# Moving bias rows and a mean to GpSimd and widening the ring of batches in an attention and ternary feed-forward kernel

## The reference

```python
def ref(x, ctx, Wq, Wk, Wv, Wo, weight, bias):     # x (64, 512, 512), ctx (64, 77, 512)
    x = x + xattn(layernorm(x), ctx, Wq, Wk, Wv, Wo)
    h = layernorm(x)
    w_scale = mean(abs(weight))
    q_weight = sign(weight) * (abs(weight) > 0.5 * w_scale)
    i_scale = max(abs(h)) / 127.0
    q_input = clip(round(h / i_scale), -128.0, 127.0)
    return x + einsum('bsk,ok->bso', q_input, q_weight) * w_scale * i_scale + bias
```

## Time and profile before

| what | value |
|---|---|
| median of three runs | 1105.96 us |
| profiled execution, its own time | 1106.15 us |
| its span, first to last instruction | 1104.4 us |
| TensorE busy | 1075.2 us, 97% |
| VectorE busy | 996.0 us, 90% |
| ScalarE busy | 931.4 us, 84% |
| GpSimd busy | 861.8 us, 78% |
| DMA | 262.94 MB, mean 238 GB/s |
| feed-forward stage | from about 808 us to the end |

### The profile page before, as it was taken

One profiled execution on the slowest core, in us unless ns is written; L12 is line 12 of the kernel. 1 busy time (PEld: TensorE's weight loads), 2 busy tenths in 40 slices (PEclk: granted clock), 3 DMA queues, 4 the chain that ended last, 5 costly groups with the idle time before them and its releaser, 6 DMA issues.

```text
span 1104.4 us, 43628 instructions
## 1 busy us (share of the span) xinstructions
PE 1075.2 (97%) x14065; PEld 867.6 (79%) x14065; DVE 996.0 (90%) x1774; ACT 931.4 (84%) x2081; POOL 861.8 (78%) x1674
## 2 busy tenths in 40 slices
PE   6998999999999999999999999999989999999996
PEld 6997999999999989999999999999745555555552
DVE  4563799999999999999999999999989999999995
ACT  3565799989999999999999999999878888888883
POOL 4675899999999999999999999999844444444442
PEclk9999999999999999999999999999999999999998
DMA  8866267666666766666666753333259999999995
GB/s 281 239 161 207 81 191 218 199 212 202 209 213 191 220 189 215 198 217 204 205 213 190 221 155 115 108 106 107 88 231 364 422 423 425 426 425 404 400 425 225
DMA packets 114615, 262.94 MB, mean 238 GB/s; under 512 B 59913, under 2 KB 71369, under 8 KB 94098
## 3 DMA queue, kind: packets, MB, share of 16 engines
q1 hardware_dynamic: 114002, 262.16, 68.7%
q10 hardware_dynamic: 576, 0.33, 0.1%
HBM read 139.79 MB, written 122.64 MB: 238 GB/s over the span
## 4 chain that ended last, share of the span: by engine, by line
DVE 45%; PE 36%; issue 15%; DVEq 2%; ACT 1%; DMA 0%; POOL 0%; SPq 0%; ACTq 0%; POOLq 0%
DVE x_sb L1110 15%; PE pT_ps L1539 10%; PE sc_ps L1539 10%; DVE mx_sb L1094 9%; DVE bn_sb L1127 6%; DVE bn_sb L1143 6%; PE y_ps L1287 5%; DVE amax L1116 3%; DVE rinv_sb L1088 2%; PE xT_ps L1276 2%; DVE e_sb L1099 2%; PE xT_ps L1525 1%; PE y_ps L1525 1%; PE sc_ps L1548 1%; PE pT_ps L1548 1%
## 5 line engine op out<-in xcount | busy, mean ns | idle before, releaser
L1452 PEld LDWEIGHTS xT_ps<-wqs,xT_sb 128*128 128x128 f32 x2048 | 239.0, 192 | 47.8 <-ACT xT_sb L867 47.7
L1452 PE MATMUL xT_ps<-wqs,xT_sb 128*128 128x128 f32 x2048 | 263.6, 282 | 2.1 <-ACT xT_sb L867 2.1
L741 POOL TENSOR_TENSOR x_sb<-x_sb,mean (+1 forms) x128 | 133.0, 1039 | 154.3 <-DVE q16T_sb L1222 154.3
L1110 DVE SCALAR_TENSOR_TENSOR x_sb<-x_sb,mv_sb,y_ps 128x512 f32 (+1 forms) x252 | 174.9, 735 | 0.1
L1410 PE MATMUL pT_ps<-v_blk,pT_sb 128*128 128x102 f32 (+1 forms) x1280 | 161.5, 273 | 0.2 <-ACT pT_sb L843 0.2
L836 ACT ACTIVATE sq_sb<-x_sb 128x512 bf16 (+1 forms) x256 | 160.7, 628 | 1.0 <-DVE x_sb L1110 0.6
L850 ACT ACTIVATE e_sb<-e_sb,rs_sb 128x308 f32<-128x308 f32 x256 | 127.3, 544 | 36.6 <-DVE e_sb L1099 36.0
L1116 DVE TENSOR_REDUCE amax<-x_sb (+1 forms) x128 | 154.8, 1210 | 0.0
L1410 PEld LDWEIGHTS pT_ps<-v_blk,pT_sb 128*128 128x128 f32 x1280 | 153.2, 192 | 1.0 <-ACT pT_sb L843 1.0
L867 ACT ACTIVATE xT_sb<-xT_ps 128x1024 f32<-128x1024 f32 x128 | 131.2, 1025 | 2.5 <-PE xT_ps L1354 2.4
L1539 PE MATMUL sc_ps<-wT,q16T_sb 64*128 64x512 f16 x1024 | 132.2, 378 | 0.6 <-DVE q16T_sb L1222 0.5
(11 more groups left out here) (155 smaller groups left out, 2376.3 us busy)
## 6 DMA issues: line engine op xcount, KB each, us to landing
out_y<-x_sb SPq DMA_DIRECT2D x112, 1024.0 KB, 9.3
x_sb<-in_x SPq DMA_DIRECT2D x128, 512.0 KB, 3.9
x_sb<-out_y SPq DMA_DIRECT2D x48, 1024.0 KB, 15.0
x_sb<-in_ctx SPq DMA_DIRECT2D x38, 256.0 KB, 4.1
v_blk<-v_scr SPq DMA_DIRECT2D x128, 20.5 KB
v_scr<-x_sb SPq DMA_DIRECT2D x38, 68.0 KB, 3.4
k_blk<-k_scr SPq DMA_DIRECT2D x128, 19.2 KB, 1.8
k_scr<-x_sb SPq DMA_DIRECT2D x38, 64.0 KB, 3.5
```

What stands on the lines that cost most here:

```text
L741: pool.tensor_tensor(row, row, stat_of(mean1, j, t, back).broadcast_to([P, E]), ALU.add).then_inc(mean_01, 1)
L1110: dve.scalar_tensor_tensor(out=x1_at(kj, gj, t), in0=x_sb[:, kj // 2, 2 * (kj % 2) + t, :], scalar=mv_sb[:, kj, t, 0:1], in1=ps[:, t, :], ...
L1452: last = pe.matmul(bank[0][:, t * HD:(t + 1) * HD], xT_sb[:, t, c, :], wqs[:, c, :], start=c == 0, stop=c == EC - 1)
```

## The change

- TensorE no longer adds the bias to tiles 2 and 3. The last of the weight products ends the sum.
- The bias comes to SBUF as a tile `bias_sb` (128x512, the same row on every partition) by a DMA on SP's queue, behind all first loads. GpSimd waits for it (`bias_in`) before its first work of the stage.
- GpSimd adds the mean of tile 3 and then the bias to tiles 2 and 3 in one instruction of 1,024 elements (`add_bias`). It waits for VectorE's quantise of the next batch, and for ScalarE's mean of tile 2 (`mean_2`).
- ScalarE quantises tiles 0, 1 and 2 and adds the means of tiles 0, 1 and 2, in another order.
- VectorE quantises tile 3, two batches ahead, between the second unoffset and the additions of tiles 2 and 3. Its first 16 turns are written out, its loop begins at batch 16.
- The ring has 24 slots (`MORE` = 4), eight loads come before the stage, and the later loads shift by two.
- `dynamic_dma_scratch_size` is set to 1024 bytes. A tensor `room` keeps the space under the overlay free of the statistics.

```diff
-MORE = 2
+MORE = 4
+ROOM = 3650
...
-                    for n in range(MORE):
+                    for n in range(2):
                         first_back(KEPT + XS + n, x1_more[n])
...
+            sp.wait_ge(pv_done, NP_)
+            sp.wait_ge(mean_ready, NP_)
+            sp.wait_ge(y_done, NP_)
+            for n in range(2, MORE):
+                first_back(KEPT + XS + n, x1_more[n])
+            sp.wait_ge(pv_done, NP_)
+            sp.dma_start(bias_sb[:, :], fb.unsqueeze(0).broadcast_to([P, E])).then_inc(bias_in, 16)
...
+            pool.wait_ge(bias_in, 16)
             pool.wait_ge(mean_ready, NP_)
 
-            def add_mean(g, k, back):
+            def add_bias(g, k, back):
...
-                for t in range(2):
-                    pool.wait_ge(qT2_copied, 2 * j + t + 1)
-                    row = x1_sb[:, bass.ds(x1_turn(g, k) + t * E, E)]
-                    pool.tensor_tensor(row, row, stat_of(mean1, j, t, back).broadcast_to([P, E]),
-                                       ALU.add).then_inc(mean_01, 1)
+                pool.wait_ge(qT2_copied, 2 * j + 2)
+                if not (isinstance(j, int) and j == B - 1):
+                    pool.wait_ge(quant_3, j + 2)
+                row = x1_sb[:, bass.ds(x1_turn(g, k) + 3 * E, E)]
+                pool.tensor_tensor(row, row, stat_of(mean1, j, 3, back).broadcast_to([P, E]), ALU.add).then_inc(mean_3, 1)
+                pool.wait_ge(mean_2, j + 1)
+                pool.wait_ge(mean_3, j + 1)
+                rows = x1_sb[:, bass.ds(x1_turn(g, k) + 2 * E, 2 * E)].rearrange("p (t e) -> p t e", t=2)
+                pool.tensor_tensor(rows, rows, bias_sb[:, :].unsqueeze(1).broadcast_to([P, 2, E]),
+                                   ALU.add).then_inc(mean_23, 2)
...
@@ scalar, turn @@
+                if left > 1:
+                    add_mean(g + (k + 1) // XS, (k + 1) % XS, (0,), mean_back)
                 if left > 2:
                     quantise(g + (k + 2) // XS, (k + 2) % XS, back)
                 if left > 1:
-                    add_mean(g + (k + 1) // XS, (k + 1) % XS, 2, mean_back)
+                    add_mean(g + (k + 1) // XS, (k + 1) % XS, (1, 2), mean_back)
                 if left > 2:
                     quantise_2(g + (k + 2) // XS, (k + 2) % XS, back)
-                if left > 1:
-                    add_mean(g + (k + 1) // XS, (k + 1) % XS, 3, mean_back)
...
@@ vector @@
+            def quantise(g, k, back, t=3):
...
+                at_least(dve, qT2_done, 2 * j)
+                dve.tensor_scalar(qm_sb[:, t // 2, 1, :], x1_sb[:, bass.ds(x1_turn(g, k) + t * E, E)],
+                                  rs2_of(j, t, back), MAGIC, ALU.mult, ALU.add)\
+                   .then_inc(quant_3 if t == 3 else quant_first, 1)
...
+                    if m == 1 and left > 2:
+                        quantise(g + (k + 2) // XS, (k + 2) % XS, back)
                     for t in range(2):
                         add(g, k, 2 * m + t)
...
@@ tensor @@
-                if second:
+                if second and m == 1:
+
+                    last.then_inc(ffn_done, 1)
+                elif second:
...
-    nc = bacc.Bacc("TRN2", target_bir_lowering=False, num_devices=1)
+    nc = bacc.Bacc("TRN2", target_bir_lowering=False, num_devices=1, dynamic_dma_scratch_size=1024)
```

More of the change, by code:

```diff
@@ L141, in build @@
                 nc.sbuf_tensor("qm_sb", [P, 2, 2, E], F32) as qm_sb, \
[L142 removed]
+                nc.sbuf_tensor("q16T_sb", [P, 2 * TPB, EC, P], F16) as q16T_sb, \
+                nc.sbuf_tensor("bias_sb", [P, E], F32) as bias_sb:
             pass
@@ L165, in build @@
         oT_sb = sb("oT_sb", [P, P], F32R)
-        sq_sb = sb("sq_sb", [P, E], BF16)
         v_blk = sb("v_blk", [P, 2, CHUNKS, 2, max(HEADS_OF), VC])
         wst = sb("wst", [P, 2, E], F32R)
+        sq_sb = sb("sq_sb", [P, E], BF16)
+        sb("room", [P, ROOM])
         bn_sb = sb("bn_sb", [P, 2, 2, 6])
@@ L260, in build @@
         x1_in = [sem(f"x1_in{n}") for n in range(XS)]
+        bias_in, mean_2, mean_3 = (sem(n) for n in ("bias_in", "mean_2", "mean_3"))
         x1_more = [sem(f"x1_more{n}") for n in range(MORE)]
@@ L928, in quantise, with quantise_2, add_mean @@
                                    bias=MAGIC, scale=rs2_of(j, t, back)).then_inc(quant_01, 1)
-            def quantise_2(g, k, back, ts=(2, 3)):
+            def quantise_2(g, k, back):
                 j = g * XS + k
                 at_least(act, qT2_done, 2 * j)
+                act.activation(qm_sb[:, 1, 0, :], x1_sb[:, bass.ds(x1_turn(g, k) + 2 * E, E)], ACT.Copy,
+                               bias=MAGIC, scale=rs2_of(j, 2, back)).then_inc(quant_2, 1)
+            def add_mean(g, k, ts, back):
+                j = g * XS + k
                 for t in ts:
[L936 to L946, removed]
+                    if t == 1 and isinstance(j, int) and j == 0:
+                        act.wait_ge(quant_first, 1)
+                    row = x1_sb[:, bass.ds(x1_turn(g, k) + t * E, E)]
+                    act.activation(row, row, ACT.Identity, bias=stat_of(mean1, j, t, back))\
+                       .then_inc(mean_2 if t == 2 else mean_01, 1)
             def turn(g, k, back):
@@ L1234, in add, with turn @@
                                          op1=ALU.add).then_inc(sum_done_t, 1)
[L1236 to L1241, removed]
+            def quantise(g, k, back, t=3):
+                j = g * XS + k
+                if back:
+                    dve.wait_ge(x1_in[k], (g - KEPT_TURNS) * 16 + 16)
+                at_least(dve, qT2_done, 2 * j)
+                dve.tensor_scalar(qm_sb[:, t // 2, 1, :], x1_sb[:, bass.ds(x1_turn(g, k) + t * E, E)],
+                                  rs2_of(j, t, back), MAGIC, ALU.mult, ALU.add)\
+                   .then_inc(quant_3 if t == 3 else quant_first, 1)
+            def turn(g, k, back):
                 j = g * XS + k
@@ L1252, in _ @@
             dve.wait_ge(scale_ready, 1)
-            quantise_first(1)
-            quantise_first(3)
+            quantise(0, 0, False, 1)
+            quantise(0, 0, False)
             unoffset(0, 0, 0)
@@ L1257, in _ @@
             bias_rows()
-            with dve.Fori(0, B // XS - 1) as g:
+            quantise(0, 1, False)
+            for j in range(KEPT):
+                turn(j // XS, j % XS, j + 2 >= KEPT)
+            with dve.Fori(KEPT_TURNS, B // XS - 1) as g:
                 for k in range(XS):
-                    turn(g, k)
+                    turn(g, k, True)
             for j in range(B - XS, B):
-                turn(j // XS, j % XS)
+                turn(j // XS, j % XS, True)
         @block.tensor
@@ L1539, in ffn @@
                         last = pe.matmul(bank[4 + t][:, :], q16T_sb[rows, 4 * par + t, c, :], wT[rows, c, :],
-                                         start=second == 0 and c == 0, stop=False)
+                                         start=second == 0 and c == 0, stop=bool(second and m == 1 and c == EC - 1))
                         if c == EC - 1 and not second:
                             last.then_inc(ffn_half, 1)
-                if second:
+                if second and m == 1:
+                    last.then_inc(ffn_done, 1)
+                elif second:
                     if isinstance(j, int) and j == 0:
```

30 lines of the change are left out of this document (17 added, 13 removed).

## The result

The changed kernel takes 1105.89 us in the median of 21 runs (1104.33 to 1108.44), the kernel before 1104.55 us in 21 runs on the same chips. The ratio is 1.0014, with a 95% interval of 1.0008 to 1.0021: 1.3 us slower, which is under the 0.2% that I called no change. I had forecast 3.8 us less, so the forecast was wrong, although the time lies within my wide range of 1099 to 1111. The profiled execution took 1105.92 us, with a span of 1103.9.

What follows compares the result with a forecast made beforehand. TensorE was taken to bound the second stage, then VectorE at 4.28 us a batch; a late first batch, 61 such periods, two of 4.2 and 0.9 us for GpSimd gave -3.8 us: 1102.2 us from 1105.96, range 1099 to 1111.

Steps and rivals of the forecast that it cites:

- What bounds the kernel: Second stage, from about 808 us: TensorE sets the pace at 4.41 us a batch; loads are far ahead, DMA does not.
- What follows the last addition: End of the second stage: the stretch from 1095.94 to the end at 1104.4 us keeps its length.
- the ring buys nothing: Ring of 24 slots in the second stage: nobody waits for it, and it costs only the late bias tile.
- TensorE, the gain: Second stage: one of two bias pairs goes, 0.21 us a batch, 4.41 to 4.20 us; alone 13.4 us, not granted.
- VectorE, the next bound: Second stage: VectorE gains one quantise of 0.40 us and needs 4.28 us a batch, covering TensorE's 4.20.
- GpSimd, close behind: Second stage: bias addition of 2.27 us, round of 3.95 us unrolled, 4.19 rolled, under 4.28; 0.9 us added for 44 batches.
- The first batch, a loss: Stage start: bias tile lands near 816.4 us, so batch 0's third addition starts at 820.3 in place of 816.47.
- The sum of the computation: Second stage: 820.3 plus 61 periods of 4.28 and two of 4.2 gives 1089.8 against 1094.53; with GpSimd's 0.9, -3.8 us.
- A DMA-bound end: End of the second stage: case in which stores land later than now; time near 1106 us, chance under 0.02.
- Rival 2: Second stage: hand-overs between TensorE, VectorE and GpSimd eat the rest, period 4.35 us, time 1105.6, no change; chance 0.20.
- Rival 1: Second stage: GpSimd becomes the bound; gain gone at an addition of 2.47 us, 1111.9 us at 2.6; chance 0.23.
- rival 3: Stage start: bias tile in before 813, no loss, third addition starts at 817.6, time 1099.5 us; chance 0.09.

Runs made afterwards that it cites:

- before_half_back: The kernel before, with each of the 42 later loads bringing back only tiles 0 and 1 of its batch; 1101.35 us, ratio 0.9965.
- ring24_only: The kernel before with the ring of 24, two more first loads and the scratch of 1,024 bytes, computation untouched; 1101.03 us, ratio 0.9964.
- early_bias: The changed kernel with the bias tile loaded in the preparation instead of behind the eight first loads; 1101.32 us, ratio 0.9967.

## Why the prediction was wrong, point by point

- **What bounds the kernel: wrong in part.** "so DMA does not set the pace; TensorE does" holds for the pace of the batches. It does not hold for the end. Before, (S to A) + 5.8 = 292.9 us, but the stage lasted 296.9: DMA already held the end back by 4.1 us. `before_half_back` and `ring24_only` took these 4 us away without touching the computation. I went by the waits of the compute engines; the wait that counted was SP's for the last stores, behind the last addition, of 5.1 us before and 9.1 us after.
- **The step that failed: "What follows the last addition (1095.94 to the end at 1104.4) stays"**, with its twin "Nobody waits for it: the ring buys nothing". I took the mean DMA share of 0.83 from 1075 to 1080 for a backlog that ends. It is a mean of 16 engines; one of them was still behind, by 7 us at that time. A to E grew from 9.87 to 13.78 us, 3.9 us, as much as the whole forecast gain of 3.8. And the ring, put at nothing, is worth 4 us alone.
- **TensorE, the gain; VectorE, the next bound: right.** 4.27 us a period (forecast 4.28), VectorE at 50.00 of 50. The quantise costs 0.44 us from start to start in place of 0.40.
- **GpSimd, close behind: right in effect, its round too short.** The bias addition takes 2.37 us, where I took 2.27 and had 2.385 from the rows. From the Trainium skill's 2.6 cycles an element (GPSIMD Engine Reference, "3.1 Elementwise — side-by-side cycle accounting") I had an estimate of 2.4 us; the trace agrees. The quantise takes 517 ns in the mean of the rolled loop and 473 in the written-out turns. In the period shown it begins 0.24 us before the addition's recorded end and is 0.51 us long in place of 0.47. So the two do meet, and it costs 0.04 us. GpSimd's round from one quantise through mean and addition to the addition's recorded end is 0.84 + 1.29 + 2.37 = 4.50 us in the rolled loop, not 4.19: it is over VectorE's 4.28 and over the 4.39 at which I had the gain gone. The period stayed at 4.27 because VectorE did not wait for the recorded end. The Trainium skill (SBUF — State Buffer, "Who interferes with whom") has the later of the two blocked fully; that would have added the 0.24 us that were left, and the trace shows 0.04. Recorded ends on GpSimd are rough, so this speaks against a full block here and does not refute it.
- **The first batch, a loss: right in kind, short in size.** The bias tile let GpSimd start at 816.22, 10.2 us after S, where the forecast of 816.4 was 8.9 after the S of the kernel before. The 0.5 us for the tile's completion in that sum had no row; the tile's completions come from 814.50 to 816.15. The third addition comes 13.75 us after S, forecast 12.8. I left out the restart at the lower clock, 2.4 us. `early_bias` took 6.1 us out of S to A, all of the stall and the restart.
- **The sum of the computation: near by luck of signs.** Forecast S to A 283.2 us, measured 284.1: the restart of 2.4 us and 0.9 us more at the start, against 61 periods of 4.26 us without the 0.9 us for GpSimd, and a shorter end (8.0 in place of 8.4 us).
- **The rivals.** "A DMA-bound end would show stores landing later than now" stood there with a chance under 0.02. It is what happened. The rows for it were there before the prediction and I gave them no weight: this window of the kernel before, and the 5.1 us in the list of SP's waits.

```profile
1100.00:1104.00 4.00, 0.00 (x0) 0.00 (x0) 0.00 (x0) 0.00 (x0) 0.00 (x0) 0.50 0.05 23
...
SPq L557 <- DMA out_y<-x_sb: 7.5, 2, 5.1
```

Rival 2 has 1105.6 us, next to the measured time, by a period of 4.35 us; the period is 4.27, so that is chance. Rival 1's condition, an addition of over 2.47 us, did not come (2.37), and rival 3's tile before 813 did not either. The chances of forecast and rivals add up to 1.01.

## What to carry to other kernels

Before a faster computation is credited, read what follows the last instruction: a DMA share of one sixteenth there meant that one DMA engine set the end, which neither the compute engines' waits nor the mean share of the steady part showed. Then what counted was how much the stage had still to move after its first store, and how soon the first stores and loads went out. The new division of work was worth 9.0 us where half of the read-back was left out, nothing with 22 slots, and with 24 slots nothing over the ring alone that the times can show. Together with a start that waits for a late small load the change came out at nothing, and with that load moved to the preparation at 0.9967, where the ring alone has 0.9964.

## What the runs showed of the hardware

- With equal transfers of 128 rows of 8 KB, one of the 16 DMA engines is some 8 us behind the others at the end of the changed kernel's stage of 298 us (0.06 from 1095 to 1103). In the full stretch it falls behind by 0.2 to 0.3 us with each store and not with the loads (before and after, 860 to 1020 us). Why, and whether it is always the same one, stays open.
- Its last packets of 8 KB follow one another every 0.306 us without a pause.
- A VectorE quantise of 128x512 from SBUF to SBUF that began 0.24 us before the recorded end of a GpSimd addition took 0.51 us in place of 0.47.
- After 5.19 us without work TensorE's granted clock was 0.50 from 820 to 825 and 0.83 in the next 5 us.
- The shortest distance from the start of the last pair of additions to the end of the span is 5.76 to 5.81 us in five kernels.
- The attention stage, the same code in all kernels, ends at one of two places, 805.1 to 806.1 or 807.2 to 807.5 us; in the times of `ring24_only` the executions fall in two groups as far apart, 1099.6 to 1099.9 and 1102.2 us. Most of the spread between executions may come from this.
